# A two-layer fused kernel: which of two engines rounds to fp8 and splits the factors in its first phase

## The chip, the cores and the metric

The kernel runs on one core of a Trainium2 chip. The metric is the device time of one execution in microseconds; the median of three runs of the kernel before is 2216.24 us (2215.17 to 2216.98). The engines are named as in the profile: PE (TensorE, matrix products), DVE (VectorE), ACT (ScalarE), POOL (GpSimd) and SP (SyncE, which issues the DMAs here).

## The reference

x has 4 x 1024 rows of 1024 columns. Four sublayers follow one another, each with a residual: `x = x + tanh(g) * f(layernorm(x))`.

```python
# first: both operands are rounded to fp8, with a factor for each block
amax = max(|xb|) over 128 columns of a row          # 128x128 for ctx
q = (xb * (448 / safe)).astype(float8_e4m3fn)        # safe = max(amax, eps)
xq = q * (safe / 448)
out = einsum('emk,enk->emn', xq, wq)                 # wq: ctx, in the same way
# second: rms norm, 8-bit activations with one scale for all of x, ternary weights
# third: attention over 8 heads, with ctx as keys and values
# fourth: 8 experts of rank 128, the best two of each row are taken
```

## The kernel before

The work is cut into 32 tiles of 128 rows, 8 to a batch. A first phase does the first sublayer and prepares the weights; it has to be over before the second starts, since the second sublayer quantises with one maximum over all of x. The second phase does the other three sublayers. The edit touches only the first phase.

In the first phase one loop, `for j in range(FIRST, LAST + 1)` (from -12 to 33), is written out by hand for every engine: in turn j each engine does its steps for different tiles, in the order of its program, and semaphores join the engines. A tile n of x goes through these steps (`j + k` means that the step is done in turn j for tile j + k):

- SP loads it (j + 5). DVE takes mean and variance (`x_stats`, j + 4, L971 and L977), POOL makes the inverse deviation from these with two small operations (`x_rstd`, j + 4, L469 and L471), and ACT subtracts the mean (`centre`).
- DVE takes the maximum of each block of 128 columns and makes the factors from it (`x_max`, j + 3, L1007 to L1015). POOL makes the factors of the way back and splits them into a high and a low part (`x_factors`, j + 3, five operations on 8 columns, L476 to L484). ACT scales the eight blocks (`x_scale`).
- The rounding to fp8 is done in f32: a step is added and subtracted again. DVE (`x_round_start`, j + 2) masks the exponents (L982), makes the step of them (L985) and adds it (L987); POOL (`x_round`, j + 2, L490) subtracts it and writes f16. The step lies in one buffer, so the next tile's mask waits for POOL's subtraction.
- The rounded tile is multiplied by the high and the low part of its factors: ACT does the high half (`x_high`, j + 1), DVE the low one (`x_low`, j + 1, L1022). SP transposes both by DMA (`turn_x`, j + 1), PE multiplies (`product`), DVE adds the residual and takes the next statistics (`finish_x1`, j - 1, L1080). ACT and DVE take a maximum for the second sublayer (`x1_abs`, `x1_max`, L1087).

A tile of ctx goes the same way without statistics: `c_max` (j + 20, L1038), `c_scale` (ACT), `c_round_start` on DVE (j + 9, the same L982 to L987) and `c_round` on POOL (L496), `c_high` and `c_low` (both ACT, for the first batch `c_low` is DVE's, L1028). Three times, in turns -3, 5 and 13, DVE makes the factors of a batch of ctx (`c_factors`), for which it waits for PE. In turns 10 to 21 DVE reduces two tiles of weights (`weight_stat`, L1092), and from turn 24 on it rounds and splits the weights (`ternary_round`, `weight_low`). SP's order for a turn puts the loads of the weights ahead of `turn_x`, and these wait for `weight_stat` or `weight_low` of the same turn.

Of the kernel before, what the change touches and what calls it, by code (L numbers as in the profile page):

```python
# [9 lines left out]
KB = D // P  # L10
# [50 lines left out]
def flamingo_two_layers(nc, x, ctx_in, g_xattn, g_ffn, w0, gamma, router_w, wa, wb, out):  # L61
# [8 lines left out]
    with ExitStack() as stack:  # L70
# [69 lines left out]
        xd, xt1, xt2 = small(KB), small(KB), small(KB)  # L140
# [73 lines left out]
        x_d, x_hi, x_lo, x_turned = signal("x_d", 5), signal("x_hi"), signal("x_lo"), signals("x_turned", 2, 32)  # L214
# [239 lines left out]
        def _(pool):  # L454
# [18 lines left out]
            def x_factors(n):  # L473

                pool.wait_ge(x_am.sem, x_am.at(n, 2))
                pool.tensor_scalar(xd[:], xsafe[:, n % 2], -AMP / FP8_MAX, None, ALU.mult).then_inc(x_d.sem, 1)  # L476
                pool.wait_ge(x_d.sem, x_d.at(n, 1))
                pool.tensor_scalar(xt1[:], xd[:], SPLIT7, None, ALU.mult).then_inc(x_d.sem, 1)
                pool.wait_ge(x_d.sem, x_d.at(n, 2))
                pool.tensor_tensor(xt2[:], xt1[:], xd[:], ALU.subtract).then_inc(x_d.sem, 1)  # L480
                pool.wait_ge(x_d.sem, x_d.at(n, 3))
                pool.tensor_tensor(xdh[:, n % 4], xt1[:], xt2[:], ALU.subtract).then_inc(x_d.sem, 1)
                pool.wait_ge(x_d.sem, x_d.at(n, 4))
                pool.tensor_tensor(xdl[:, n % 4], xd[:], xdh[:, n % 4], ALU.subtract).then_inc(x_d.sem, 1)  # L484

            def x_round(n):
                pool.wait_ge(x_u.sem, x_u.at(n))
                after(pool, x_hi, n - 2)
                after(pool, x_lo, n - 2)
                pool.tensor_tensor(XQ[n % 2], XC[n % 3][:], XSTEP, ALU.subtract).then_inc(x_q.sem, 1)  # L490

            def c_round(m):
                pool.wait_ge(c_u.sem, c_u.at(m))
                after(pool, c_hi, m - 2)
                after(pool, c_lo, m - 2)
                pool.tensor_tensor(CQ[m % 2], C[m % 3], CSTEP, ALU.subtract).then_inc(c_q.sem, 1)  # L496
# [23 lines left out]
            for j in range(FIRST, LAST + 1):  # L520
                if is_x(j + 4):
                    x_rstd(j + 4)
                if is_x(j + 3):
                    x_factors(j + 3)
                if j in (-3, 5, 13):
                    c_tables((j + 11) // PER_BATCH)
                if j == PREP - 1:
                    weight_factors()
                if is_x(j + 2):
                    x_round(j + 2)  # L530
                if is_c(j + C_ROUND):
                    c_round(j + C_ROUND)
# [72 lines left out]
        def _(act):  # L605
# [23 lines left out]
            def x_high(n):  # L629
                act.wait_ge(x_q.sem, x_q.at(n))  # L630
                act.wait_ge(x_d.sem, x_d.at(n, 4))
                if n >= 2:
                    act.wait_ge(x_turned[n % 2].sem, x_turned[n % 2].at(n // 2 - 1))
                by_block(XHL[n % 2][0], XQ[n % 2], xdh[:, n % 4], x_hi)
# [334 lines left out]
        def _(dve):  # L969
# [9 lines left out]
            def round_start(v, s, v_sig, s_sig, u_sig, n):  # L979

                dve.wait_ge(v_sig.sem, v_sig.at(n))
                dve.tensor_scalar(s.bitcast(U16), v.bitcast(U16)[:, 1::2], EXP_MASK, None,  # L982
                                  ALU.bitwise_and).then_inc(s_sig.sem, 1)
                dve.wait_ge(s_sig.sem, s_sig.at(n, 1))
                dve.tensor_scalar(s, s, FP8_MIN_NORMAL, ROUND_FP8, ALU.max, ALU.mult).then_inc(s_sig.sem, 1)  # L985
                dve.wait_ge(s_sig.sem, s_sig.at(n))
                dve.tensor_tensor(v, v, s, ALU.add).then_inc(u_sig.sem, 1)  # L987

            def x_round_start(n):
                after(dve, x_q, n - 1)  # L990
                if n == 0:
                    dve.wait_ge(c_v.sem, c_v.at(PER_BATCH - 1))
                round_start(XC[n % 3][:], XSTEP, x_v, x_s, x_u, n)

            def c_round_start(m):
                after(dve, c_q, m - 1)
                round_start(C[m % 3], CSTEP, c_v, c_s, c_u, m)
# [19 lines left out]
            def x_low(n):  # L1017
                dve.wait_ge(x_q.sem, x_q.at(n))
                dve.wait_ge(x_d.sem, x_d.at(n))
                if n >= 2:  # L1020
                    dve.wait_ge(x_turned[n % 2].sem, x_turned[n % 2].at(n // 2 - 1))
                dve.tensor_tensor(blocks(XHL[n % 2][1]), blocks(XQ[n % 2]), spread(xdl[:, n % 4]), ALU.mult)\  # L1022
                   .then_inc(x_lo.sem, 1)
# [121 lines left out]
            for j in range(FIRST, LAST + 1):  # L1145
# [3 lines left out]
                if is_x(j + 1):  # L1149
                    x_low(j + 1)  # L1150
                if is_x(j + 3):
                    x_max(j + 3)
                if is_x(j + 4):
# [5 lines left out]
                if is_x(j + 2):  # L1159
                    x_round_start(j + 2)  # L1160
                if j in (-3, 5, 13):
                    c_factors((j + 11) // PER_BATCH)
                if is_c(j + C_ROUND):
                    c_round_start(j + C_ROUND)
# [222 lines left out]
```

## Time and profile before

| what | value |
|---|---|
| median of three runs | 2216.24 us |
| the profiled execution | 2218.67 us |
| its span | 2216.9 us |
| busy in the span: PE | 1866.9 us (84%) |
| DVE | 1668.4 us (75%) |
| ACT | 1360.1 us (61%) |
| POOL | 858.3 us (39%) |
| end of the first phase | about 607 us |

Busy time is the time in which an instruction is under way on an engine, its waiting for a memory port included; waiting for a semaphore counts as idle time. The times of a timeline start at the span's start.

### The profile page before, as it was taken

To read this page: it belongs to the slowest core of one execution; us is meant where nothing else is said; L and a number is where in the kernel's file an instruction comes from. 1 tells how busy PE (TensorE), PEld (TensorE's weight loads), DVE (VectorE), ACT (ScalarE), POOL (GpSimd) and SP (SyncE) were. 2 spreads that over 40 slices of the span, in tenths; PEclk is the share of its full clock that TensorE was granted. 3 is DMA by queue.
4 is the path that set the end of the run, shared out by engine and by line. 5 is a ranking of instruction groups with operands and counts; after the bars stand their busy time and mean duration, and the time that the engine had idled before them with its cause. 6 is when DMAs were issued, how large, how long until landed. Compare 5 with 4: busy or idle time off the path is not lost.

```text
span 2216.9 us, 26479 instructions
## 1 busy us (share of the span) xinstructions
PE 1866.9 (84%) x8716; PEld 826.1 (37%) x8716; DVE 1668.4 (75%) x2348; ACT 1360.1 (61%) x2587; POOL 858.3 (39%) x1256
## 2 busy tenths in 40 slices
PE   0186667777746999999999999999999999999997
PEld 0032223332312444444444444444444444444443
DVE  8999989999546777777767777777777767777661
ACT  5798969977225565565565565565565565565650
POOL 2666646654023333333333433333333333433320
PEclk9998887898967999999999999999999999999998
DMA  7778769978637778878888878788778878778781
GB/s 217 193 208 198 199 176 233 250 182 213 183 92 140 150 154 170 159 156 168 158 156 165 161 162 163 158 162 161 161 155 168 158 156 163 164 163 163 133 150 41
DMA packets 963529, 369.33 MB, mean 167 GB/s; under 512 B 915136, under 2 KB 931520, under 8 KB 963392
## 3 DMA queue, kind: packets, MB, share of 16 engines
q1 hardware_dynamic: 963392, 367.64, 76.7%
q8 instruction: 69, 1.13, 0.2%
q14 instruction: 68, 0.56, 0.1%
HBM read 105.42 MB, written 33.55 MB: 63 GB/s over the span
## 4 chain that ended last, share of the span: by engine, by line
DVE 38%; issue 17%; ACT 16%; PE 13%; POOL 9%; DMA 6%; SPq 1%; POOLq 0%; ACTq 0%; DVEq 0%
ACT slot L716 7%; DVE tiny L971 7%; DVE tiny L1240 7%; POOL tiny L572 4%; ACT arena L708 4%; DMA slot<-slot 3%; POOL tiny L570 3%; DVE slot L1244 3%; ACT tiny L702 2%; PE accs L848 2%; PE sc L865 2%; PE accs L850 2%; PE accs L849 2%; DMA probs<-slot 2%; DVE slot L1022 2%
## 5 line engine op out<-in xcount | busy, mean ns | idle before, releaser
L1244 DVE SCALAR_TENSOR_TENSOR slot<-arena,tiny,slot 128x1024 f16<-128x1024 f32 x256 | 328.2, 1282 | 283.2 <-ACT slot L716 283.1
L865 PE MATMUL sc<-arena,slot 128*128 128x512 f16 x1536 | 381.3, 385 | 31.0 <-ACT arena L708 21.3
L716 ACT ACTIVATE slot<-arena,tiny 128x1024 f16<-128x1024 f32 x256 | 293.7, 1147 | 182.0 <-POOL tiny L572 166.6
L570 POOL TENSOR_SCALAR tiny<-tiny 128x1 f32<-128x1 f32 x256 | 99.3, 388 | 704.5 <-ACT arena L708 704.5
L1240 DVE TENSOR_REDUCE tiny<-sc 128x1 f32<-128x1024 f32 x256 | 308.5, 1206 | 57.8 <-PE sc L865 57.8
L708 ACT ACTIVATE arena<-sc,tiny,head_tab 128x1024 f32<-128x1024 f32 x256 | 308.4, 1205 | 8.6
L702 ACT ACTIVATE tiny<-tiny,head_tab 128x1 f32<-128x1 f32 x256 | 74.1, 289 | 359.4 <-DVE tiny L1240 358.4
L810 PE MATMUL sc<-probs,slot 128*128 128x512 f16 x768 | 190.0, 412 | 89.1 <-DMA slot<-slot 78.9
L865 PEld LDWEIGHTS sc<-arena,slot 128*128 128x128 f16 x1536 | 151.2, 99 | 219.7 <-ACT arena L708 25.9
L810 PE MATMUL sc<-wa_hi,slot 128*128 128x512 f16 x512 | 145.8, 406 | 78.1 <-DMA wa_lo<-wb_lo 46.8
L848 PE MATMUL accs<-wb_hi,slot 128*128 128x512 f16 x512 | 195.1, 381 | 7.5 <-DMA slot<-slot 7.5
L848 PE MATMUL accs<-wa_hi,slot 128*128 128x512 f16 x512 | 199.7, 390 | 0.0
L850 PE MATMUL accs<-wa_hi,slot 128*128 128x512 f16 x512 | 199.4, 389 | 0.0
L849 PE MATMUL accs<-wa_lo,slot 128*128 128x512 f16 x512 | 199.0, 389 | 0.0
L881 PE MATMUL accs<-probs,arena 128*128 128x512 f16 x512 | 195.0, 381 | 4.1 <-issue 3.9
L849 PE MATMUL accs<-wb_lo,slot 128*128 128x512 f16 x512 | 195.0, 381 | 0.0
L850 PE MATMUL accs<-wb_hi,slot 128*128 128x512 f16 x512 | 194.8, 380 | 0.0
L883 PE MATMUL accs<-probs,arena 128*128 128x512 f16 x512 | 194.8, 380 | 0.0
L882 PE MATMUL accs<-probs,arena 128*128 128x512 f16 x512 | 194.6, 380 | 0.0
L572 POOL TENSOR_TENSOR tiny<-tiny,neg_one 128x1 f32<-128x1 f32 x256 | 161.3, 630 | 21.3
L810 PEld LDWEIGHTS sc<-probs,slot 128*128 128x128 f16 x768 | 79.0, 105 | 199.4 <-DMA slot<-slot 85.3
L612 ACT ACTIVATE wb_lo<-wb_lo,slot 128x128 f16<-128x128 f16 x448 | 136.2, 386 | 14.7 <-POOL wb_lo L496 12.9
(178 smaller groups left out, 3181.0 us busy)
## 6 DMA issues: line engine op xcount, KB each, us to landing
wb_hi<-in_ctx SPq DMA_DIRECT2D x36, 512.0 KB, 4.7
arena<-in_x SPq DMA_DIRECT2D x32, 512.0 KB, 3.6
x_scratch<-arena SPq DMA_DIRECT2D x32, 512.0 KB, 3.1
slot<-x_scratch SPq DMA_DIRECT2D x32, 512.0 KB, 3.8
slot<-in_ctx SPq DMA_DIRECT2D x32, 512.0 KB, 4.1
out<-arena SPq DMA_DIRECT2D x32, 512.0 KB, 3.4
slot<-in_L_ffn_weight SPq DMA_DIRECT2D x16, 512.0 KB, 3.4
slot<-in_L_ffn_Wa SPq DMA_DIRECT2D x16, 512.0 KB, 4.8
```

What stands on the lines that cost most here:

```text
L572: pool.tensor_tensor(rinv[c % 2][:], rsum[c % 2][:], neg_one[:], ALU.pow).then_inc(s_ri.sem, 1)
L708: act.activation(PF[c % 2], sc[:, c % 2, :], ACT.Exp, bias=nbias[c % 2][:], scale=head_tab[:, n, 1:2], accum_out=rsum[c % 2][:]).then_inc( ...
L716: act.activation(PH[c % 2], PF[c % 2], ACT.Identity, scale=rinv[c % 2][:]).then_inc(s_ph.sem, 1)
L810: mm = pe.matmul(sc[:, j % 2, h * HALF:(h + 1) * HALF], lhs[:, cols], rhs[:, k, h * HALF:(h + 1) * HALF], start=start, stop=stop)
L848: pe.matmul(accs[:, a, :], lhs_hi, r_hi[:, k, cols], start=k == 0, stop=False)
L849: pe.matmul(accs[:, a, :], lhs_hi, r_lo[:, k, cols], start=False, stop=False)
L850: mm = pe.matmul(accs[:, a, :], lhs_lo, r_hi[:, k, cols], start=False, stop=k == KB - 1)
L865: mm = pe.matmul(sc[:, c % 2, h * HALF:(h + 1) * HALF], q[i][:, c * P:(c + 1) * P], k[j][:, h * HALF:(h + 1) * HALF], start=start, stop=stop)
L881: pe.matmul(accs[:, ACC_V, :], v[0][:, cols], PT[:, h, j, :], start=j == 0, stop=False)
L883: mm = pe.matmul(accs[:, ACC_V, :], v[1][:, cols], PT[:, h, j, :], start=False, stop=j == KB - 1)
L1240: dve.tensor_reduce(nmx[c % 2][:], sc[:, c % 2, :], AX.X, ALU.max, negate=True).then_inc(s_mx.sem, 1)
L1244: dve.scalar_tensor_tensor(out=PL[c % 2], in0=PF[c % 2], scalar=rinv[c % 2][:], in1=PH[c % 2], op0=ALU.mult, op1=ALU.subtract).then_inc(s_ ...
```

## The change

- Both passes of each rounding are POOL's: the addition of the step goes from DVE (L987) to POOL, ahead of the subtraction, for x and for ctx. DVE keeps the mask and the step.
- The low half of x (`x_low`) goes from DVE to POOL.
- The factors of x (`x_factors`) go from POOL to DVE, behind `x_max`. There are four instructions instead of five, since two of them do two steps each.
- The order within a turn is changed on both engines. On DVE: the steps of x and ctx first (with `c_factors` between them), then `x_max` and `x_factors`, `x_stats`, `x1_max`, the rest as before. On POOL: `x_low`, `x_round`, `x_rstd`, the tables of ctx, `c_round`.

```diff
 (POOL)
+            def x_low(n):
+                pool.wait_ge(x_q.sem, x_q.at(n))
+                pool.wait_ge(x_d.sem, x_d.at(n))
+                if n >= 2:
+                    pool.wait_ge(x_turned[n % 2].sem, x_turned[n % 2].at(n // 2 - 1))
+                pool.tensor_tensor(blocks(XHL[n % 2][1]), blocks(XQ[n % 2]), spread(xdl[:, n % 4]), ALU.mult)\
+                    .then_inc(x_lo.sem, 1)
             def x_round(n):
+                pool.wait_ge(x_s.sem, x_s.at(n))
+                pool.tensor_tensor(XC[n % 3][:], XC[n % 3][:], XSTEP, ALU.add).then_inc(x_u.sem, 1)
                 pool.wait_ge(x_u.sem, x_u.at(n))
...
             def c_round(m):
+                pool.wait_ge(c_s.sem, c_s.at(m))
+                pool.tensor_tensor(C[m % 3], C[m % 3], CSTEP, ALU.add).then_inc(c_u.sem, 1)
                 pool.wait_ge(c_u.sem, c_u.at(m))
...
             for j in range(FIRST, LAST + 1):
+                if is_x(j + 1):
+                    x_low(j + 1)
+                if is_x(j + 2):
+                    x_round(j + 2)
                 if is_x(j + 4):
                     x_rstd(j + 4)
-                if is_x(j + 3):
-                    x_factors(j + 3)
                 if j in (-3, 5, 13):
                     c_tables((j + 11) // PER_BATCH)
                 if j == PREP - 1:
                     weight_factors()
-                if is_x(j + 2):
-                    x_round(j + 2)
                 if is_c(j + C_ROUND):
                     c_round(j + C_ROUND)
 (DVE)
-            def round_start(v, s, v_sig, s_sig, u_sig, n):
+            def rounding_step(v, s, v_sig, s_sig, n):
...
-                dve.wait_ge(s_sig.sem, s_sig.at(n))
-                dve.tensor_tensor(v, v, s, ALU.add).then_inc(u_sig.sem, 1)
...
+            def x_factors(n):
+                dh, dl = xdh[:, n % 4], xdl[:, n % 4]
+                dve.tensor_scalar(xd[:], xsafe[:, n % 2], -AMP / FP8_MAX, None, ALU.mult).then_inc(x_d.sem, 1)
+                dve.wait_ge(x_d.sem, x_d.at(n, 1))
+                dve.scalar_tensor_tensor(out=xt2[:], in0=xd[:], scalar=SPLIT7, in1=xd[:], op0=ALU.mult,
+                                         op1=ALU.subtract).then_inc(x_d.sem, 1)
+                dve.wait_ge(x_d.sem, x_d.at(n, 2))
+                dve.scalar_tensor_tensor(out=dh, in0=xd[:], scalar=SPLIT7, in1=xt2[:], op0=ALU.mult,
+                                         op1=ALU.subtract).then_inc(x_d.sem, 1)
+                dve.wait_ge(x_d.sem, x_d.at(n, 3))
+                dve.tensor_tensor(dl, xd[:], dh, ALU.subtract).then_inc(x_d.sem, 1)
...
-                if is_x(j + 1):
-                    x_low(j + 1)
+                if is_x(j + 2):
+                    x_step(j + 2)
+                if j in (-3, 5, 13):
+                    c_factors((j + 11) // PER_BATCH)
+                if is_c(j + C_ROUND):
+                    c_step(j + C_ROUND)
                 if is_x(j + 3):
                     x_max(j + 3)
+                    x_factors(j + 3)
                 if is_x(j + 4):
                     x_stats(j + 4)
                 if is_x(j - 2):
                     x1_max(j - 2)
                 if j == PREP - 1:
                     weight_factors()
-                if is_x(j + 2):
-                    x_round_start(j + 2)
-                if j in (-3, 5, 13):
-                    c_factors((j + 11) // PER_BATCH)
-                if is_c(j + C_ROUND):
-                    c_round_start(j + C_ROUND)
                 if is_x(j - 1):
                     finish_x1(j - 1)
```

## Rows read from the trace of the kernel before

**Rows 1.** Busy us by stretch: PE, weight load, DVE, ACT, POOL, then clock, DMA.
```profile
200.00:250.00 50.00, 36.98 (x158) 15.58 (x157) 48.82 (x71) 46.59 (x141) 34.71 (x33) 0.92 0.89 222
607.00:2216.90 1609.90, 1489.32 (x7170) 667.23 (x7170) 1117.74 (x1548) 905.46 (x1281) 547.95 (x930) 0.97 0.77 152
```

**Rows 2.** Timeline of one pass, DVE and one POOL row: start us, us, engine, operation.
```profile
201.16 1.22 DVE L987 TENSOR_TENSOR wb_hi<-wb_hi,slot 128x1024 f32<-128x1024 f32 x1
202.31 1.28 DVE L1080 SCALAR_TENSOR_TENSOR arena<-sc,tiny,arena 128x1024 f32<-128x1024 f32 x1
...
205.07 2.12 POOL L496 TENSOR_TENSOR wb_lo<-wb_hi,slot 128x1024 f16<-128x1024 f32 x1
206.15 2.13 DVE L1022 TENSOR_TENSOR slot<-slot 128x1024 f16<-128x1024 f16 x1
208.20 1.21 DVE L1007 TENSOR_REDUCE tiny<-slot 128x8 f32<-128x1024 f32 x1
...
210.08 1.28 DVE L971 BATCH_NORM_STATS2 tiny<-arena 128x6 f32<-128x512 f32 x2
...
211.52 1.17 DVE L1087 CUSTOM_DVE_ANT_0 slot<-slot 128x1024 f32<-128x1024 f32 x1
...
216.15 1.22 DVE L987 TENSOR_TENSOR wb_hi<-wb_hi,slot 128x1024 f32<-128x1024 f32 x1
```

**Rows 3.** Timeline of the same pass on ACT.
```profile
205.18 1.15 ACT L663 ACTIVATE slot<-arena,row_tab 128x1024 f32<-128x1024 f32 x1 [0.20 <-DVE row_tab L977]
206.24 2.43 ACT L612 ACTIVATE slot<-slot 128x128 f16<-128x128 f16 x8
208.57 2.43 ACT L612 ACTIVATE wb_lo<-wb_lo,slot 128x128 f16<-128x128 f16 x8
```

**Rows 4.** Groups of instructions by line, 100 to 550 us: busy us, mean ns.
```profile
L490 POOL TENSOR_TENSOR slot<-slot,arena 128x1024 f16<-128x1024 f32 x29 | 61.8, 2130 | 0.3 <-issue 0.2
...
L982 DVE TENSOR_SCALAR arena<-slot 128x1024 uint16<-128x1024 uint16 x29 | 20.3, 701 | 0.0
...
L985 DVE TENSOR_SCALAR arena<-arena 128x1024 bf16<-128x1024 bf16 x29 | 12.4, 427 | 1.0
...
L1066 DVE SCALAR_TENSOR_TENSOR slot<-slot 128x64 f32<-128x64 f32 x2 | 0.5, 226 | 0.1
```

**Rows 5.** Timeline of DVE and POOL at three places.
```profile
96.06 2.74 DVE L1028 TENSOR_TENSOR wb_lo<-wb_lo,slot 128x1024 f16<-128x1024 f16 x1
97.68 3.10 POOL L496 TENSOR_TENSOR wb_lo<-wb_hi,slot 128x1024 f16<-128x1024 f32 x1
98.73 3.14 DVE L1022 TENSOR_TENSOR slot<-slot 128x1024 f16<-128x1024 f16 x1
...
184.66 2.12 POOL L490 TENSOR_TENSOR slot<-slot,arena 128x1024 f16<-128x1024 f32 x1
184.68 2.38 DVE L985 TENSOR_SCALAR slot<-slot 128x1024 bf16<-128x1024 bf16 x1
...
464.88 1.75 DVE L1109 TENSOR_SCALAR slot<-slot,tiny 4x128 f32<-4x128 f32 x1
```

**Rows 6.** Groups of instructions by line on POOL, whole span.
```profile
L551 POOL TENSOR_TENSOR slot<-slot 128x1024 f16<-128x1024 f32 x32 | 73.2, 2289 | 70.4 <-ACT slot L726 70.4
```

**Rows 7.** Timeline of DVE: `finish_x1` of tiles 0, 21 and 27, and `c_factors` in pass 13.
```profile
123.54 1.28 DVE L1080 SCALAR_TENSOR_TENSOR arena<-sc,tiny,arena 128x1024 f32<-128x1024 f32 x1
...
317.43 0.23 DVE L1053 TENSOR_SCALAR slot<-accs 128x64 f32<-128x64 f32 x1 [7.42 <-PE accs L800]
...
461.65 1.28 DVE L1080 SCALAR_TENSOR_TENSOR arena<-sc,tiny,arena 128x1024 f32<-128x1024 f32 x1
...
547.26 1.28 DVE L1080 SCALAR_TENSOR_TENSOR arena<-sc,tiny,arena 128x1024 f32<-128x1024 f32 x1 [0.80 <-PE sc L810]
```

**Rows 8.** Timeline of DVE: sums of two ctx tiles ahead of x.
```profile
36.09 1.23 DVE L987 TENSOR_TENSOR wb_hi<-wb_hi,slot 128x1024 f32<-128x1024 f32 x1
...
41.70 1.22 DVE L987 TENSOR_TENSOR wb_hi<-wb_hi,slot 128x1024 f32<-128x1024 f32 x1
```

More of the change, by code:

```diff
@@ L139, in flamingo_two_layers @@
         xam, xsafe, xrec, xk = small(KB), sb("xsafe", [P, 2, KB]), small(KB), sb("xk", [P, 2, KB])
-        xd, xt1, xt2 = small(KB), small(KB), small(KB)
+        xd, xt2 = small(KB), small(KB)
         xdh, xdl = (slot[13][:, 192 + i * 32:224 + i * 32].rearrange("p (a k) -> p a k", a=4) for i in range(2))
@@ L213, in flamingo_two_layers @@
                                          signal("x_q"))
-        x_d, x_hi, x_lo, x_turned = signal("x_d", 5), signal("x_hi"), signal("x_lo"), signals("x_turned", 2, 32)
+        x_d, x_hi, x_lo, x_turned = signal("x_d", 4), signal("x_hi"), signal("x_lo"), signals("x_turned", 2, 32)
         mm1, e_x1, x1_out, e_st, e_abs, e_max = (signal("mm1"), signal("e_x1"), signal("x1_out", 16), signal("e_st", 3),
@@ L471, in x_rstd @@
                 pool.tensor_tensor(xrstd[:, i:i + 1], xa_[:], neg_half[:, 0:1], ALU.pow).then_inc(x_rs.sem, 1)
[L473 to L484, printed above, removed]
+            def x_low(n):
[5 more added lines that the diff above has]
+                    .then_inc(x_lo.sem, 1)
             def x_round(n):
+                pool.wait_ge(x_s.sem, x_s.at(n))
+                pool.tensor_tensor(XC[n % 3][:], XC[n % 3][:], XSTEP, ALU.add).then_inc(x_u.sem, 1)
                 pool.wait_ge(x_u.sem, x_u.at(n))
@@ L630, in x_high @@
                 act.wait_ge(x_q.sem, x_q.at(n))
-                act.wait_ge(x_d.sem, x_d.at(n, 4))
+                act.wait_ge(x_d.sem, x_d.at(n, 3))
                 if n >= 2:
@@ L985, in round_start, with x_step @@
                 dve.tensor_scalar(s, s, FP8_MIN_NORMAL, ROUND_FP8, ALU.max, ALU.mult).then_inc(s_sig.sem, 1)
-                dve.wait_ge(s_sig.sem, s_sig.at(n))
-                dve.tensor_tensor(v, v, s, ALU.add).then_inc(u_sig.sem, 1)
-            def x_round_start(n):
+            def x_step(n):
                 after(dve, x_q, n - 1)
@@ L992, in x_round_start, with c_step @@
                     dve.wait_ge(c_v.sem, c_v.at(PER_BATCH - 1))
-                round_start(XC[n % 3][:], XSTEP, x_v, x_s, x_u, n)
-            def c_round_start(m):
+                rounding_step(XC[n % 3][:], XSTEP, x_v, x_s, n)
+            def c_step(m):
                 after(dve, c_q, m - 1)
-                round_start(C[m % 3], CSTEP, c_v, c_s, c_u, m)
+                rounding_step(C[m % 3], CSTEP, c_v, c_s, m)
             def x_stats(n):
@@ L1015, in x_max @@
                 dve.tensor_scalar(xk[:, i], xrec[:], xrstd[:, i:i + 1], FP8_MAX, ALU.mult, ALU.mult).then_inc(x_k.sem, 1)
[L1017 to L1023, printed above, removed]
+            def x_factors(n):
[9 more added lines that the diff above has]
+                dve.tensor_tensor(dl, xd[:], dh, ALU.subtract).then_inc(x_d.sem, 1)
             def c_low(m):
```

## The prediction

> **What bounds the kernel now.** I read the busy time by stretch first. The edit touches only the first phase, the first 607 us of the span. In 200 to 250 us DVE is busy 48.8 of 50 us, ACT 46.6, POOL 34.7 and PE 37.0 [rows 1]: DVE sets the pace and ACT is close behind. In the second phase, which the edit leaves as it is, DVE is busy 1117.7 of 1609.9 us [rows 1]; a gain or a loss of the first phase therefore moves the end one for one.
>
> Then the timeline of one pass. By pass j I mean one turn of the loop over j. From sum to sum of a ctx tile (L987 at 201.16 and at 216.15) a pass takes 14.99 us, and DVE's pieces fill it [rows 2]: ctx sum 1.15, `finish_x1` and `c_max` together 3.84 (202.31 to 206.15), `x_low` 2.05, `x_max` 1.88, `x_stats` 1.44, `x1_max` 1.10, and the rounding of x and ctx up to 216.15. ACT's pass has five groups of eight block scalings, 2.33 us apart, and two operations of some 1.06 us [rows 3]: 5 x 2.33 + 2.1 = 13.8 us. That is the floor to which a faster DVE could bring the pass, 1.2 us below today.
>
> Last, and decisive here, how DVE and POOL stand in each other's way. At 184.64 DVE had just written the step of a ctx tile. Between its two step instructions there is a gap of some 0.03 us. POOL started its difference in it (184.66, 2.12 us), and DVE's next instruction, which takes 0.43 us alone [rows 4], took 2.38, ending 0.28 after POOL [rows 5]. In the group from 96 us the two take turns: DVE's L1028 ends at 98.80, POOL's L496, begun at 97.68, takes 3.10 instead of some 2.13, and DVE's L1022, begun at 98.73, takes 3.14 and ends 1.09 after it [rows 5]. Even 128 elements on four partitions wait: L1109 took 1.75 us beside POOL's L496 [rows 5]. Instructions of another kind don't wait: POOL's L496 at 205.07 lies beside `c_max`, and DVE gets to its next instruction, L1022, at 206.15 as ever; that one then stands for POOL and ends 1.09 after it [rows 2]. So the wait is not a slowing of both; one stands until the other's instruction is through.
>
> The Trainium skill ("SBUF — State Buffer", Who interferes with whom) says the same of two kinds of DVE instruction, those in a two-port mode and those with two SBUF inputs: each and a GpSimd operation exclude one another for a whole instruction. By that rule a `tensor_scalar` of 8 elements waits too, which no row here shows; by it my sum stands, without it a pass would be some 0.9 us shorter (below).
>
> **What the change moves, per pass.** From DVE go two sums (1.15 each) and `x_low` (2.05, of which some 0.9 is waiting for POOL); to it come four instructions on 8 columns, some 0.25 us apart as those on 64 columns (0.23 each) [rows 2, 4]. DVE's own work: 14.99 - 2.3 - 2.05 + 1.0 = 11.7 us, rounded up for the last spacing. From POOL go five small operations; to it come three large ones. No row shows POOL doing these three; its large two-tensor operations take 2.13 us (L490) and 2.29 (L551, with waiting) [rows 4, 6], so I take 2.1 from start to start. The f16 input and the spread factor of `x_low` may make it dearer; 2.29 each is my upper end, 2.1 the lower one. POOL's pass: 5 x 2.13 + the pair of `x_rstd`, about 0.9 = 11.6 us. Each engine alone would be faster than ACT's 13.8. What decides is the order in which they exclude one another.
>
> **A pass of the changed kernel, walked.** Clock 0 is the end of `x_stats`, for which POOL's `x_rstd` waits, and behind it in POOL's order everything else.
> - 0 to 1.1: DVE's `x1_max`. POOL's `x_rstd` pair stands behind it and ends at 1.8. DVE goes on with `finish_x1` and `c_max` to 4.95 (from pass 10 with two weight statistics to 7.2), which POOL doesn't disturb. POOL: ctx sum 1.9 to 4.0, ctx difference 4.1 to 6.2.
> - DVE's first mask (x) waits for it: 6.2 to 6.85. In the gap behind it POOL's `x_low` enters: 6.9 to 8.95. DVE scales the step 9.0 to 9.4 and runs straight into the ctx mask, to 10.05. Here POOL's x sum enters, 10.05 to 12.2. DVE's ctx scale: to 12.6.
> - DVE's block maximum runs beside POOL's x difference (12.6 to 14.7), but `xsafe` waits for its end. Then seven small instructions, 14.7 to 16.4, and `x_stats` to 17.8.
>
> So 17.8 us a pass: DVE's 11.7 and 6 us of standing for POOL (1.2 + 2.1 + 2.1 + 1.0, less rounding). ACT has 4 us to spare in it, PE more. The weight statistics of passes 10 to 21 are hidden: they fall where DVE would wait anyway.
>
> **The sum.** `finish_x1` of tile 0 is at 123.54, of tile 21 at 461.65, of tile 27 at 547.26 [rows 7].
> - 21 passes between the first two, 338.1 us now. Nineteen become 17.8. In pass 5 `c_factors` adds some 2.7 of its own: 20.5. In pass 13 DVE waits for PE at `c_factors` until 317.43 (7.42 of it idle) [rows 7], some 15.3 behind the end of pass 12, as the transposes are issued only behind the weight statistics of that pass. `c_factors` now stands ahead of `x_max`, so more is left behind it: 15.3 + 2.7 + 11.5 = 29.5, against 27.4 now and against 17.8: 30.6 with the shift of phase. Together 19 x 17.8 + 20.5 + 30.6 = 389.3: +51.
> - Six passes to tile 27, 85.6 us now. No ctx tile is rounded any more. The first takes 16.2, the second 12.2; the four with weights: 13.2 of DVE's work, and 3.0 waiting for POOL's x sum and difference at `x_max` = 16.2. Together 93.2: +7.6.
> - Before tile 0: ctx alone takes 5.61 a pass (36.09 to 41.70) [rows 8]. Now: step 1.15, sum 2.1, difference 2.2, and `c_low` 1.1 between these two = 6.5; five passes, +4.5. Passes -2 to 0, 43.4 us together in the timeline now, become by the same walk 17.6, 17.6 (with `c_low` on DVE) and 16.5: +8.3. Passes -4 and -3, where the ctx step and `c_factors` now stand ahead of x's statistics, so that these come later and `x_rstd` with all behind it on POOL waits: +5, an estimate from the same walk. Together +18.
> - The last four tiles wait for transposes and PE, whose place behind `weight_low` in SP's order doesn't change: 0, give or take 3.
>
> Sum +76.5 us. Before's profiled execution took 2218.67 us with a span of 2216.9 and some 1.8 around it, 2.4 above the median of 2216.24; I put the change on the median: 2292.7, rounded 2292.
>
> **Bounds.** If the three new operations of POOL cost 2.29 instead of 2.1, a pass gains 0.2 for each: 28 passes x 0.6 = +16. If small instructions of 8 columns with one input don't wait, -0.9 x 27 = -24. If each of the 28 passes has one handover less than I walked (2.1 us), -59: 2233. If it has half of one more, +29: 2321.
>
> **The rivals.**
> - **The pair is packed well** (0.13). The order falls so that DVE's own long work (6.4 us of statistics and maxima) covers POOL. Then only the sum of what excludes one another counts: 5 x 2.13, 0.5 of `x_rstd`, four step instructions 2.3, `x1_max` 1.1, the small ones 1.1 = 15.6 a pass, against 15.2 on average: 27 x 0.4 = +11: 2227. Against it: `x_rstd` stands ahead of the ctx rounding in POOL's order, so POOL idles 3 us in each pass, and DVE's step instructions stand in a row.
> - **The other side: the relief counts** (0.08). DVE gets its turn without waiting for more than 2 us a pass, 11.7 + 2.1 = 13.8, ACT's floor. 20 passes x 1.2 less, the rest unchanged: 2192. It decides from the point where DVE's waits stay under 3.3 us a pass. For it: DVE's busy time today. Against it: rows 5, in which a single gap cost 1.95 us.
> - **The three operations are dearer than any of POOL's today** (0.12), for instance by 0.5 each, 28 passes x 1.5 = +42 more: 2334.
> - **It changes nothing that can be told** (0.02): waits and relief cancel, 2216.
> - My forecast: 0.65.
>
> Measured medians of this kernel lie within 0.1%; 0.2% is what can be told from no change. Slower by more: 0.65 + 0.12 + 0.13 less 0.01 = 0.89; same 0.03; faster 0.08. The range, 2232 to 2326, leaves out the gain and the dearest case.
>
> **What would show it.** In the timeline of the changed kernel: passes of 17 to 18 us in mid phase; the bfloat16 scalings of the step (0.43 alone) at some 2 us on average; POOL's five large operations some 2.1 each, with POOL idle ahead of `x_rstd`; `xsafe` behind the end of POOL's x difference; DVE's busy share still high, as its waits are booked as busy; the second phase as long as before. I'm wrong if the scalings keep 0.43 us, or if a pass takes less than 15 us.

## The result and the profile after

The changed kernel took 2255.11 us (median of four runs, 2244.87 to 2257.19), the kernel before 2216.61 on the same chip (2215.17 to 2218.73): 1.0171 times as long, with a 95% interval of 1.0149 to 1.0192. It is slower, as forecast; the loss of 38.5 us is half of the 76 forecast. The profiled execution took 2254.88 us, its span is 2253.1, 36.2 longer than before's 2216.9.

Busy time by stretch, as in [rows 1]: the same 50 us, and the second phase.

```profile
200.00:250.00 50.00, 28.99 (x111) 11.69 (x110) 48.82 (x69) 41.60 (x126) 37.96 (x25) 0.80 0.70 172
645.50:2253.10 1607.60, 1484.66 (x7171) 666.16 (x7170) 1120.23 (x1552) 904.37 (x1281) 543.80 (x930) 0.97 0.77 152
```

DVE is still booked as busy for 48.82 of 50 us, though three of its large instructions a pass are gone. ACT fell from 46.59 to 41.60 and PE from 36.98 to 28.99: less work goes through in the same time. So what counts as DVE's busy time is to a good part standing. One pass on DVE shows where; it answers to [rows 2], from the end of one `x_stats` over the LayerNorm statistics behind `finish_x1` (256.70) to the next `x_stats` (L981 is the mask, L984 the scaling of a step, L1004 to L1025 the block maximum and the factors).

```profile
254.17 0.21 DVE L976 BATCH_NORM_AGGREGATE xmv<-tiny 128x2 f32<-128x12 f32 x1
...
256.70 1.29 DVE L970 BATCH_NORM_STATS2 tiny<-arena 128x6 f32<-128x512 f32 x2
...
258.15 1.17 DVE L1040 TENSOR_REDUCE slot<-wb_hi 128x8 f32<-128x1024 f32 x1
259.23 1.83 DVE L981 TENSOR_SCALAR arena<-slot 128x1024 uint16<-128x1024 uint16 x1
261.10 2.00 DVE L984 TENSOR_SCALAR arena<-arena 128x1024 bf16<-128x1024 bf16 x1
263.02 0.68 DVE L981 TENSOR_SCALAR slot<-wb_hi 128x1024 uint16<-128x1024 uint16 x1
263.73 2.23 DVE L984 TENSOR_SCALAR slot<-slot 128x1024 bf16<-128x1024 bf16 x1
265.89 1.20 DVE L1004 TENSOR_REDUCE tiny<-slot 128x8 f32<-128x1024 f32 x1
267.13 0.86 DVE L1008 TENSOR_SCALAR xsafe<-tiny 128x8 f32<-128x8 f32 x1
...
268.26 0.23 DVE L1012 TENSOR_SCALAR xk<-tiny 128x8 f32<-128x8 f32 x1
268.40 0.16 DVE L1017 TENSOR_SCALAR tiny<-xsafe 128x8 f32<-128x8 f32 x1
268.60 0.17 DVE L1019 SCALAR_TENSOR_TENSOR tiny<-tiny 128x8 f32<-128x8 f32 x1
...
269.08 1.28 DVE L970 BATCH_NORM_STATS2 tiny<-arena 128x6 f32<-128x512 f32 x2
270.40 0.21 DVE L976 BATCH_NORM_AGGREGATE xmv<-tiny 128x2 f32<-128x12 f32 x1
```

And the same pass on POOL: `x_rstd` (L469, L471), ctx sum and difference (L491, L495), `x_low` (L478), x sum and difference (L483, L487).

```profile
254.46 1.08 POOL L469 TENSOR_SCALAR tiny<-xmv 128x1 f32<-128x1 f32 x1 [2.74 <-DVE xmv L976]
...
256.16 2.14 POOL L491 TENSOR_TENSOR wb_hi<-wb_hi,slot 128x1024 f32<-128x1024 f32 x1
258.37 2.14 POOL L495 TENSOR_TENSOR wb_lo<-wb_hi,slot 128x1024 f16<-128x1024 f32 x1
260.46 2.35 POOL L478 TENSOR_TENSOR slot<-slot 128x1024 f16<-128x1024 f16 x1
263.17 2.51 POOL L483 TENSOR_TENSOR slot<-slot,arena 128x1024 f32<-128x1024 f32 x1 [0.36 <-DVE arena L984]
265.76 2.20 POOL L487 TENSOR_TENSOR slot<-slot,arena 128x1024 f16<-128x1024 f32 x1
```

Read them side by side. POOL's L495 ends at 260.51, and the mask, begun at 259.23, ends only at 261.06: 1.83 us instead of 0.68. Behind it POOL's `x_low` is through first, and the scaling of x's step takes 2.00 instead of 0.43. The second mask slips in at its own 0.68; then POOL's x sum gets its turn, and the scaling of the ctx step takes 2.23. The block maximum is undisturbed (1.20), and `xsafe`, on 8 columns, stands for POOL's L487 until 267.96. These four stand for 1.15 + 1.57 + 1.80 + 0.63 = 5.15 us in a pass of 16.23, from one end of `x_stats` (254.38) to the next (270.61). Before, one instruction a pass stood, `x_low`, for 0.92 (2.13 in [rows 2] where it takes 1.21 undisturbed), and from pass 10 on, where the weight statistics lie ahead of `x_low`, none. This is no single pass: the groups, 100 to 550 us, answer to [rows 4].

```profile
L984 DVE TENSOR_SCALAR slot<-slot 128x1024 bf16<-128x1024 bf16 x24 | 49.9, 2080 | 0.8
L984 DVE TENSOR_SCALAR arena<-arena 128x1024 bf16<-128x1024 bf16 x26 | 41.5, 1596 | 0.9
L981 DVE TENSOR_SCALAR arena<-slot 128x1024 uint16<-128x1024 uint16 x26 | 34.9, 1342 | 0.0
L1008 DVE TENSOR_SCALAR xsafe<-tiny 128x8 f32<-128x8 f32 x27 | 22.3, 827 | 1.0
```

Last, `finish_x1` of tiles 0, 21 and 27, and `c_factors` of pass 13, beside [rows 7].

```profile
136.85 1.25 DVE L1082 SCALAR_TENSOR_TENSOR arena<-sc,tiny,arena 128x1024 f32<-128x1024 f32 x1
...
343.18 0.22 DVE L1055 TENSOR_SCALAR slot<-accs 128x64 f32<-128x64 f32 x1 [13.92 <-PE accs L799]
...
499.44 1.28 DVE L1082 SCALAR_TENSOR_TENSOR arena<-sc,tiny,arena 128x1024 f32<-128x1024 f32 x1
...
588.03 1.28 DVE L1082 SCALAR_TENSOR_TENSOR arena<-sc,tiny,arena 128x1024 f32<-128x1024 f32 x1
```

| stretch | before, us | after, us | difference | forecast |
|---|---|---|---|---|
| start of the span to tile 0 | 123.5 | 136.9 | +13.3 | +18 |
| tile 0 to 21 | 338.1 | 362.6 | +24.5 | +51 |
| tile 21 to 27 | 85.6 | 88.6 | +3.0 | +7.6 |
| tile 27 to 31 | 56.8 | 57.5 | +0.8 | 0 |
| tile 31 to the end | 1612.9 | 1607.5 | -5.4 | 0 |

The last line is not the edit's. In the ten further kernels below, whose second phase is the same code, it took 1603.9 to 1611.1 us in one execution each. Before's 1612.9 is the longest of all.

### The profile page after: what moved, and what is told of

Read it like the earlier page. It is cut to its first block, busy times and chain, and to the rows that moved or that the text cites. A ratio compares the mean times of both kernels' runs of the same rounds, so it can differ in the third digit from the quotient of the medians.

```text
span 2253.1 us, 26447 instructions
## 1 busy us (share of the span) xinstructions
PE 1866.8 (83%) x8716; PEld 825.8 (37%) x8716; DVE 1689.4 (75%) x2380; ACT 1357.6 (60%) x2587; POOL 956.1 (42%) x1192
## 4 chain that ended last, share of the span: by engine, by line
DVE 37%; issue 19%; ACT 16%; PE 12%; POOL 9%; DMA 6%; SPq 1%; POOLq 0%; ACTq 0%; DVEq 0%
ACT slot L715 7%; DVE tiny L1241 7%; DVE tiny L970 7%; POOL tiny L571 4%; ACT arena L707 4%; DMA slot<-slot 3%; POOL tiny L569 3%; DVE slot L1245 2%; ACT tiny L701 2%; DMA probs<-slot 2%; PE sc L864 2%; DVE arena L1253 2%; DVE slot L1228 2%; PE sc L809 2%; PE accs L847 2%
## 5 line engine op out<-in xcount | busy, mean ns | idle before, releaser
L611 ACT ACTIVATE slot<-slot,xk 128x128 f32<-128x128 f32 x256 | 78.2, 388 | 119.0 <-DVE xk L1012 119.0
```

## The experiments

Theory A is the prediction's: DVE and POOL exclude one another for a whole instruction, and what a pass loses is set by which of POOL's operations is ready in the gaps between DVE's short ones. Theory B: POOL's added work by itself makes the loss, wherever it stands. Theory C: neither; the new order with its chain of handed-over results costs what it costs through waits for data. D and E came up on the way and are told where they are tested. The table is the ledger of all of them, from one steady pass each, `finish_x1` to `finish_x1` around 200 to 265 us: "standing" is the sum of what DVE's instructions took above their undisturbed duration in the same kernel, "own" is the rest of the pass, without idle time. The last column compares with runs of the kernel before on the same chip.

| kernel | pass | own | standing, and on what | median, us | ratio to before, 95% |
|---|---|---|---|---|---|
| before | 14.98 | 14.06 | 0.92: `x_low` | | |
| after | 16.23 | 11.08 | 5.15: mask, both scalings, `xsafe` | 2255.11 | 1.0171 [1.0149, 1.0192] |
| a1, sums back on DVE | 16.17 | 13.61 | 2.56: mask, ctx scaling | 2252.21 | 1.0166 [1.0135, 1.0196] |
| a2, `x_low` back on DVE | 15.76 | 12.22 | 3.54: `x_low`, ctx scaling, `xsafe` | 2246.23 | 1.0136 [1.0117, 1.0156] |
| a3, masks first | 15.99 | 10.83 | 5.16: both masks, `xsafe`, `xk` | 2253.40 | 1.0174 [1.0136, 1.0213] |
| a4, one block of eight on POOL | 13.76 | 11.18 | 0; 2.58 idle for ACT | 2170.91 | 0.9799 [0.9775, 0.9823] |
| a5, order of before | 15.32 | 11.10 | 4.22: ctx scaling, `xsafe`, `xk` | 2221.73 | 1.0041 [1.0028, 1.0054] |
| b1, before in the new order | 15.86 | 14.05 | 1.81: ctx scaling | 2247.32 | 1.0141 [1.0118, 1.0164] |
| b2, before with `x_low` later | 14.09 | 14.09 | 0 | 2202.40 | 0.9952 [0.9935, 0.9969] |
| b3, b2 with the x sum on POOL | 14.61 | 12.82 | 1.79: `xsafe` | 2203.32 | 0.9956 [0.9942, 0.9970] |
| w1, b3's division, grouped | 14.24 | 12.90 | 0; 1.34 idle for ACT | 2236.69 | 1.0111 [1.0078, 1.0144] |
| w2, after's division, grouped | 16.97 | 11.19 | 3.17: `xk`, one factor; 2.61 idle for ACT | 2272.82 | 1.0271 [1.0236, 1.0305] |

In passes 14 to 21, with two weight statistics in each, the same count gives 15.2 and nothing standing for before, 12.2 and 4.0 for the changed kernel, 15.2 and 1.8 for b1, 12.2 and 3.1 for a5, 15.2 and nothing for b2.

### Is it POOL's length, or the order alone? (a4, b1)

The first takes nearly all the length out of POOL's five large operations and leaves order and semaphores of the changed kernel. Seven blocks of eight of each result are left out; the time alone is of use.

```diff
-pool.tensor_tensor(XC[n % 3][:], XC[n % 3][:], XSTEP, ALU.add)
+pool.tensor_tensor(XC[n % 3][:, 0:P], XC[n % 3][:, 0:P], XSTEP[:, 0:P], ALU.add)
 ...
```

> The changed kernel with all five large POOL operations of a turn (both sums, both differences, x_low) cut to one block of 128 columns of 1024; order, semaphores and DVE's work stay. Left out: seven blocks of eight of each of these results (they are zero or unrounded). Theory A and B: passes fall to ACT's floor of 13.8 us, 2171 us (2160 to 2185). Theory C (the new order or its semaphores cost the time, whatever POOL's operations last): a pass stays at 15 us or more, above 2205 us.

2170.91 us, as expected. The busy times of 200 to 250 us:

```profile
200.00:250.00 50.00, 37.62 (x156) 15.76 (x154) 43.16 (x85) 50.00 (x154) 14.19 (x26) 0.86 0.91 239
```

ACT is busy all the time and sets the pass, 13.8 us, the floor that [rows 3] gave. Theory C is out: the same order with the same semaphores, but short operations on POOL, doesn't hold a pass above ACT's floor. A and B had the same number here.

The second leaves POOL and DVE what they have in the kernel before and gives both the changed kernel's order.

```diff
 for j ...:      # DVE's loop; on POOL x_round and x_factors go ahead of x_rstd
+    if is_x(j + 2): x_round_start(j + 2)
+    if j in (-3, 5, 13): c_factors((j + 11) // PER_BATCH)
+    if is_c(j + C_ROUND): c_round_start(j + C_ROUND)
     if is_x(j + 3): x_max(j + 3)
 ...
-    if is_x(j + 2): x_round_start(j + 2)
-    if j in (-3, 5, 13): c_factors((j + 11) // PER_BATCH)
-    if is_c(j + C_ROUND): c_round_start(j + C_ROUND)
```

> The kernel before with its own division of the work (DVE adds the steps and does x_low, POOL the factors), but with the order of the changed kernel on DVE and POOL: steps first, then the maxima and statistics; x_round ahead of x_rstd. Theory A: POOL's x difference is now ready while DVE is between ctx mask and ctx scale, about 1.9 us of waiting, against the 0.9 us that x_low waited: passes of 15.6 us (from pass 12 on 16.8) against 15.0 and 15.2: 2246 us (2235 to 2255). Theory B (POOL's load, DVE's relief): no operation has changed sides, so 2216 us, within 5.

2247.32 us: A's number, and most of the changed kernel's loss, without one operation more on POOL than before. B is refuted as the main cause. The place, DVE and POOL (L490 is POOL's x difference, L982 and L985 mask and scaling of the ctx step):

```profile
250.41 0.69 DVE L982 TENSOR_SCALAR slot<-wb_hi 128x1024 uint16<-128x1024 uint16 x1
250.57 2.51 POOL L490 TENSOR_TENSOR slot<-slot,arena 128x1024 f16<-128x1024 f32 x1 [4.56 <-DVE slot L987]
251.13 2.23 DVE L985 TENSOR_SCALAR slot<-slot 128x1024 bf16<-128x1024 bf16 x1
...
262.81 1.22 DVE L1022 TENSOR_TENSOR slot<-slot 128x1024 f16<-128x1024 f16 x1
```

The difference, asked for at 250.57 during the mask, gets in between mask and scaling, and the scaling takes 2.23 instead of 0.43. `x_low` has lost its wait in exchange (262.81, 1.22). One handover of 0.92 was traded for one of 1.81; in the passes with weight statistics, 15.2 us before, it is the whole 1.8: 17.0.

### Undoing one part at a time (a1, a2)

```diff
 def rounding_step(v, s, v_sig, s_sig, u_sig, n):    # a1, on DVE
 ...
+    dve.wait_ge(s_sig.sem, s_sig.at(n))
+    dve.tensor_tensor(v, v, s, ALU.add).then_inc(u_sig.sem, 1)
 # and both sums deleted on POOL
```

> The changed kernel, but DVE adds the step again (both sums back on DVE), so that DVE's own work per pass is 13.9 us and POOL's falls by 4.2. Theory A (DVE and POOL exclude one another; what counts is which POOL operation is ready at the gaps between DVE's short locked instructions): the x difference now enters the gap between ctx mask and ctx scale (about 1.9 us of waiting) and x_low stands before the x mask (about 0.9), so a pass is 16.2 to 16.5 us, as long as with the sums on POOL: 2253 us (2245 to 2262). Theory B (POOL's load is the cause): most of the loss goes with the two sums, 2215 to 2225.

2252.21 us; the interval includes the changed kernel's ratio. POOL is relieved of 4.3 us a pass and DVE burdened with 2.3, and the pass moves by 0.06: own work +2.5, standing -2.6. Once more B's number (2215 to 2225) is far off.

```diff
-if is_x(j + 1): x_low(j + 1)     # head of POOL's loop
+if is_x(j + 1): x_low(j + 1)     # head of DVE's loop (a2)
```

> The changed kernel, but x_low is DVE's again, at the head of its turn. Theory A: DVE does 1.1 us more, one handover of about 2 us at the x step is gone; walked by the same rules a pass is 15.7 us against 16.2: 2244 us (2238 to 2250). Theory B (load): POOL loses one of five large operations, a third of the loss: 2242 us. Not meant to tell these two apart, but to size one handover.

2246.23 us, 2.2 over the expected. Own work +1.14, standing -1.61: the pass is 0.5 shorter, 15.76 where 15.7 was expected. Neither part of the division alone is the culprit. B had 2242 here, so this run doesn't tell the two apart; it sizes one handover.

### Can the gaps be avoided? (a3)

Theory D: the loss sits in the gap between mask and scaling; with both masks ahead of both scalings, it shrinks.

```diff
     x_mask(j + 2)
     c_mask(j + C_ROUND)
+    x_scale_step(j + 2)
+    c_scale_step(j + C_ROUND)
```

> The changed kernel with DVE's four step instructions in the order mask x, mask ctx, scale x, scale ctx, so that no instruction waits for the one just ahead of it and the four run without a gap (2.1 us in one piece). Theory A (POOL's operations only change place: x_low, x sum and x difference still have to run between the step and the statistics, now in the gaps between the small instructions on 8 columns): a pass is 16.5 us against 16.2, 2261 us (2250 to 2268). Theory D (the gaps between the step instructions are the fault): without them about 4 us a pass go, down to ACT's floor, below 2205 us.

2253.40 us: not told apart from the changed kernel, and D's number (under 2205) missed by some 50. The scalings run at 0.41 to 0.42, but the ctx mask (L981) takes 2.38 and `xk` (L1014), on 8 columns, 1.93:

```profile
259.15 1.82 DVE L981 TENSOR_SCALAR arena<-slot 128x1024 uint16<-128x1024 uint16 x1
260.38 2.35 POOL L478 TENSOR_TENSOR slot<-slot 128x1024 f16<-128x1024 f16 x1
260.90 2.38 DVE L981 TENSOR_SCALAR slot<-wb_hi 128x1024 uint16<-128x1024 uint16 x1
...
266.01 2.12 POOL L487 TENSOR_TENSOR slot<-slot,arena 128x1024 f16<-128x1024 f32 x1
266.24 1.93 DVE L1014 TENSOR_SCALAR xk<-tiny 128x8 f32<-128x8 f32 x1
```

The standing is 5.16 against 5.15: it has only moved. A had 2261 and passes of 16.5; the time lies in its range, the pass took 15.99. And the gap isn't needed. The ctx mask began at 260.90, before the x mask was through (260.97), and still stood for `x_low`, which had been standing since 260.38. Here an operation of POOL that stood already got in behind the DVE instruction it stood for, without a gap.

### The order of before with the new division (a5)

Theory E: the order alone makes the loss; then this one, with the new division in the old order, is as fast as the kernel before.

```diff
 # POOL's and DVE's loops as in the kernel before, operations as in the changed one
-    x_round(j + 2)                                       # POOL, ahead of x_rstd(j + 4)
+    x_round(j + 2)                                       # POOL, behind weight_factors
-    x_step(j + 2); c_factors(...); c_step(j + C_ROUND)   # DVE, ahead of x_max(j + 3)
+    x_step(j + 2); c_factors(...); c_step(j + C_ROUND)   # DVE, behind weight_factors
```

> The division of the changed kernel (sums and x_low on POOL, factors on DVE) in the order of the kernel before, on both engines. It completes a square of two divisions and two orders. Theory A, walked: the step instructions are through before POOL's x sum, but POOL's five large operations then run in a row to 14.0 us after x_stats, and DVE's small instructions wait for two of them: 16.0 us a pass; with the slower ctx passes at the start (6.5 against 5.6) 2244 us (2236 to 2255). Theory E (the loss of the changed kernel is that of its order alone, as b1 lost 31 us by the order alone): 2216 us, within 6.

2221.73 us, seven runs. With b1 this closes a square:

| | order of before | order of the change |
|---|---|---|
| division of before | 1 | 1.0141 |
| division of the change | 1.0041 | 1.0171 |

The order costs 1.3 to 1.4 per cent in either row; the division 0.4 in the old order. In the new one 0.3, which the intervals of b1 and of the changed kernel don't tell apart. The traces say the same: `finish_x1` of tile 31 is at 604.0 us before, 636.0 in b1, 614.2 in a5 and 645.6 in the changed kernel, so that the order costs 32.0 and 31.3 us and the division 10.2 and 9.6, in one execution each. So three quarters to four fifths of the loss come from the order, 29 to 32 us. "Order" is both engines' at once; the share of each wasn't tried. In a5 `x_low` and the factors stay where the changed kernel has them, since before has no place for them on these engines. E's number (2216, within 6) is just met, though this kernel is told apart from before. My own by A, 2244, was wrong by 22. I had walked 16.0 us; a pass takes 15.32, and 15.3 to 15.8 with weight statistics. DVE and POOL (L983 to L491 as in the changed kernel):

```profile
250.32 2.51 POOL L483 TENSOR_TENSOR slot<-slot,arena 128x1024 f32<-128x1024 f32 x1
250.88 2.23 DVE L984 TENSOR_SCALAR slot<-slot 128x1024 bf16<-128x1024 bf16 x1
...
258.11 1.30 DVE L1008 TENSOR_SCALAR xsafe<-tiny 128x8 f32<-128x8 f32 x1
259.34 1.90 POOL L478 TENSOR_TENSOR slot<-slot 128x1024 f16<-128x1024 f16 x1
259.69 1.58 DVE L1012 TENSOR_SCALAR xk<-tiny 128x8 f32<-128x8 f32 x1
```

Here `x_low` begins at 259.34, in the gap behind `xsafe`, and `xk` on 8 columns stands for it. Own work is the changed kernel's 11.1. Against before, in the same order, the new division takes 3.0 us of own work off DVE and puts 3.3 of standing on it. Against the changed kernel, what differs is that POOL's x difference, its ctx sum and the first part of its ctx difference (252.91 to 259.39, one behind the other) lie beside `finish_x1`, its statistics, `c_max` and the block maximum (253.03 to 258.08), and one standing less is left.

### Moving one step of the kernel before (b2, b3)

If the place decides, before's own 0.92 can be had without any new division: `x_low` goes behind `x_stats`, where POOL has nothing large left.

```diff
 ...                                     # POOL's x_factors also waits for its own last one
-                if is_x(j + 1):
-                    x_low(j + 1)
                 if is_x(j + 3):
                     x_max(j + 3)
                 if is_x(j + 4):
                     x_stats(j + 4)
+                if is_x(j + 1):
+                    x_low(j + 1)
```

> The kernel before with one step moved: DVE does x_low behind x_stats instead of at the head of its turn. No operation changes its engine or its length alone. Theory A: x_low no longer meets POOL's ctx difference, which now lies beside the block maxima; passes up to 9 fall from 15.0 to 14.1 us, those with weight statistics (where x_low didn't wait) stay at 15.2: 2204 us (2198 to 2211). Theory B (load): nothing, 2216 us.

2202.40 us over ten runs, against 2204 expected: faster than both kernels, and with b3 below, which can't be told from it, the fastest that computes the whole. Busy times and the pass (L491, L497 POOL's differences; L1008 block maximum; L1023 `x_low`):

```profile
200.00:250.00 50.00, 38.28 (x162) 16.44 (x163) 48.76 (x76) 49.12 (x150) 37.50 (x31) 0.90 0.90 231
```

```profile
213.19 2.13 POOL L491 TENSOR_TENSOR slot<-slot,arena 128x1024 f16<-128x1024 f32 x1
214.12 1.29 DVE L972 BATCH_NORM_STATS2 tiny<-arena 128x6 f32<-128x512 f32 x2
215.27 2.13 POOL L497 TENSOR_TENSOR wb_lo<-wb_hi,slot 128x1024 f16<-128x1024 f32 x1
215.56 1.17 DVE L1039 TENSOR_REDUCE slot<-wb_lo 128x8 f32<-128x1024 f32 x1
216.65 1.21 DVE L1008 TENSOR_REDUCE tiny<-slot 128x8 f32<-128x1024 f32 x1
...
219.97 1.21 DVE L1023 TENSOR_TENSOR slot<-slot 128x1024 f16<-128x1024 f16 x1
```

Both of POOL's large operations lie whole beside statistics and maxima, which take their usual time; `x_low` takes 1.21. Nothing of DVE's stands. In passes 14 to 21 a pass takes the 15.2 it took before, where nothing stood. With ACT at 49.12 of 50 us the next bound is reached too.

b3 gives POOL the x sum on top of that, to use DVE's undisturbed time further.

```diff
 # on top of b2; the x sum is deleted on DVE
+                pool.wait_ge(x_s.sem, x_s.at(n))                      # x_round(n) on POOL
+                pool.tensor_tensor(XC[n % 3][:], XC[n % 3][:], XSTEP, ALU.add)
 ...
-                if is_x(j + 2): x_round(j + 2)     # POOL's loop, ahead of c_round
+                if is_x(j + 2): x_round(j + 2)     # behind it
```

> b2 (the kernel before with x_low behind x_stats), and x's sum moved to POOL, where x_round now comes behind c_round, so that nothing of POOL's large work is ready before DVE's step instructions are through. Theory A: in passes with weight statistics DVE's 15.3 us fall by the sum's 1.15 and POOL's three operations (6.4 us) fit beside DVE's statistics and maxima: 14.3 us against 15.2; passes up to 9 stay at 14.1 to 14.3 (ACT's floor, and 1.4 us of waiting at xsafe): 2192 us (2185 to 2200). Theory B (each large operation moved to POOL costs): above 2202 us, the time of b2.

2203.32 us, no gain over b2, where 2192 was expected; B's number, above 2202, is met. The trace shows three things against it. In passes up to 9, `xsafe` waits for POOL's x difference (1.79), which the sum ahead of it has made later: own work -1.27, standing +1.79. In the passes with weight statistics ACT waits for that difference:

```profile
379.27 2.14 POOL L493 TENSOR_TENSOR slot<-slot,arena 128x1024 f16<-128x1024 f32 x1
380.93 0.50 DVE L1015 TENSOR_SCALAR xsafe<-tiny 128x8 f32<-128x8 f32 x1
381.44 2.44 ACT L615 ACTIVATE slot<-slot 128x128 f16<-128x128 f16 x8 [0.77 <-POOL slot L493]
```

Three large operations, 6.4 us, no longer fit beside the 5.05 us from the start of `finish_x1` to the end of the block maximum (b2: 212.81 to 217.86). Even so b3 gains 5.6 us on b2 from tile 0 to 21 (327.7 against 333.3). It loses 6.3 from tile 21 to 27 (89.2 against 82.8), where DVE waits twice for PE at the summary of the weights, 1.85 and 2.13 us; the rest of that stretch is not explained.

### Gathering all of DVE's undisturbed work (w1, w2)

In both kernels I put statistics and maxima in one run behind `finish_x1`, with POOL's large operations in one run beside them, and moved ACT's scalings to match. w1 has before's division with x's sum on POOL, as b3, and w2 the changed one.

```diff
 # DVE, tail of the loop; ahead of finish_x1 come c_factors, the ctx step and the x step
+    x_stats(j + 4); x_max(j + 3); x_low(j + 1); x1_max(j - 2)     # w1
+    x_stats(j + 4); x_max(j + 3); x_factors(j + 3); x1_max(j - 2) # w2
 # ACT: x_scale(j + 3) and centre(j + 4) moved behind the work on ctx
```

> The division of before, save that x's sum is POOL's, in an order made from theory A: DVE does ctx step and sum, x step, then all that doesn't exclude POOL in one stretch (finish_x1, ctx maximum or weight statistics, x_stats, block maximum), then the small ones, x_low and x1_max; POOL does x sum, x difference, ctx difference inside that stretch, then x_rstd and the factors; on ACT x_scale and centre go to the end of the turn. Theory A: DVE's work is 12.6 to 13.9 us a pass with little waiting, so ACT's floor of 13.8 to 14 decides: 2184 us (2176 to 2195). Theory B (every further large operation on POOL costs): above 2216 us.

> The division of the changed kernel (both sums and x_low on POOL, factors on DVE) in the same kind of order as w1. POOL's five large operations take 10.4 us in a row and meet DVE's small instructions at the end of its stretch. Theory A: 15.0 us a pass, with ctx alone 6.5 against 5.6 as in the changed kernel: 2216 us (2205 to 2228), 39 us less than the changed kernel by order alone, but no gain on before. Theory B: still near 2255 us.

Both missed, by 53 and 57 us: 2236.69 and 2272.82. In w1 nothing stands for POOL, and its steady pass is the expected 14.2. But the mask waits for ACT in each pass, and `c_factors` for PE's transposes (before: 7.4 us in all, in pass 13 [rows 7]):

```profile
200.39 0.69 DVE L986 TENSOR_SCALAR arena<-slot 128x1024 uint16<-128x1024 uint16 x1 [1.34 <-ACT slot L616]
```

```profile
L1058 DVE TENSOR_SCALAR slot<-accs 128x64 f32<-128x64 f32 x2 | 0.5, 225 | 23.3 <-PE accs L804 23.3
```

Its passes 5 and 13 take 29.9 and 32.4 us, where before has 19.8 and 29.5. In w2 the same wait for ACT is 2.6 us a pass, and two small instructions stand besides, for 3.2 us:

```profile
246.31 0.69 DVE L982 TENSOR_SCALAR arena<-slot 128x1024 uint16<-128x1024 uint16 x1 [2.61 <-ACT slot L612]
...
254.37 1.83 DVE L1013 TENSOR_SCALAR xk<-tiny 128x8 f32<-128x8 f32 x1
256.31 1.74 DVE L1020 SCALAR_TENSOR_TENSOR tiny<-tiny 128x8 f32<-128x8 f32 x1
```

But most of w1's loss lies later. It reaches tile 21 only 1.3 us behind before (462.9 against 461.7) and takes 166.9 from there to tile 31, against 142.4: `finish_x1` waits for PE, 40.4 us in all against 18.2 before, 34.9 of it from 480 us on. In w2 the same stretch takes 162.4, against 146.1 in the changed kernel. Which part of the order makes PE late wasn't tried. An order that is right for the pair DVE and POOL can be wrong for ACT and PE. B's number for w1, above 2216, is met as well, yet nothing of DVE's stands for POOL in its steady pass; w2's fits neither. So these two decide nothing between A and B, and give no gain.

## Why the prediction was right, and by what its size was off

**The bound.** Right. The loss of the first phase, 41.6 us up to `finish_x1` of tile 31, reached the end but for 5.4, which is within what the second phase varies by between executions of the same code (1603.9 to 1612.9).

**What the change moves.** DVE's own work was put at 11.7 us a pass and is 11.08. About half of that is the spacing of the small instructions: on 8 columns they start 0.20 apart (268.40, 268.60) and take 0.17, not the 0.25 taken from those on 64 columns, and the four add 0.68 and not 1.0. Most of the rest is that each sum took the gap ahead of it along: from the start of a scaling to the next mask it was 1.60 before (213.36 to 214.96) and is 0.35 without the standing, 1.25 less where 1.15 had been taken off.

**Whether small instructions wait.** No row of before showed it, and the forecast had it by the nearest, the 128 elements of [rows 5]. The trace now shows it for 8 columns: `xsafe` 0.86, in a5 `xk` 1.58, in a3 1.93, against 0.23 alone.

**The walk.** All handovers are where it put them: the mask behind POOL's ctx difference, `x_low` between mask and scaling, x sum behind the ctx mask, x difference beside the block maximum and `xsafe` behind it. Even POOL's idle time ahead of `x_rstd` is there, 2.74 against some 3. With clock 0 at the end of `x_stats` (254.38):

| end of | walk | trace |
|---|---|---|
| `x_rstd` | 1.8 | 1.81 |
| ctx difference | 6.2 | 6.13 |
| `x_low` | 8.95 | 8.43 |
| x sum | 12.2 | 11.30 |
| x difference | 14.7 | 13.58 |
| last small instruction (start of `x_stats`) | 16.4 | 14.70 |
| `x_stats` | 17.8 | 16.23 |

So the step that was off is the price of a handover, in "a pass of the changed kernel, walked". The walk let DVE stand for 1.2, 2.1, 2.1 and 1.0 us (6.4, where the sum has 6); the mask, the two scalings and `xsafe` stood for 1.15, 1.57, 1.80 and 0.63. I had let each instruction start anew, 2.1 us for POOL's operation and 0.4 for DVE's scaling behind it. But one that stood needs less than its whole time from the other's end: `x_low` ends 1.75 us after DVE's mask, where alone it takes 1.90 (a5, 259.34), x sum and difference 1.98 and 2.00 after DVE's end where 2.12 was their time in [rows 5]; the scaling of the ctx step ends 0.28 after POOL's. [Rows 5] had that last number, for L985, and I quoted it and walked with 0.4 all the same. With the rest of the walk this splits the 1.57 us between 17.8 and 16.23 so: 17.8 was 11.7 of own work and 6.1 of standing, 16.23 is 11.08 and 5.15. Standing makes 0.95 of it (0.2 of which is that `x_low` takes 1.90 even undisturbed, not 2.1), own work 0.6. The passes of 17 to 18 us that were to be seen in mid phase were therefore not seen.

**The sum.** The two passes with `c_factors` and the two behind them took 86.0 us together, forecast 86.7. The other 17 between tiles 0 and 21 took 276.6, where 17.8 each makes 302.6: the 26 us too much of this term. The wait for PE in pass 13 grew from 7.42 to 13.92, as the argument on `c_factors` had it. Ahead of tile 0 the ctx passes were right (6.45 us from mask to mask, 6.5 forecast); the 4.7 too much lie, by subtraction, in the passes with x, which have the same handovers; I did not go through them one by one. From tile 21 to 27, four passes with weights took 60.3 where I had 64.8. In the first of them (527.75 to 543.38) DVE stood for 2.5 us, not 3.0; but the last took 13.75 where I had 16.2, and that one I did not go through.

**The bounds.** The large operations were not dearer (2.12 undisturbed, `x_low` 1.90), and "one handover less", 2233, did not come about; the truth was the same number of handovers, each cheaper, which was none of my cases. That the range held 2255 is partly luck: its lower end was made for a case that did not occur.

**The rivals.** "The pair is packed well" was refuted for this order (15.6 a pass) and is what a5 shows, at 15.32. "The relief counts" fell: DVE's waits were to stay under 3.3 us and are 5.15. What I hadn't seen is that the order, and not the division, carries most of the loss; the prediction argued from both at once, and didn't walk them apart.

## What to carry to other kernels

Where two engines exclude one another for whole instructions, keep a ledger of one pass: own work, standing, idle time, and for each standing the other engine's operation behind it. Then place the other engine's long operations beside work that doesn't exclude them, before moving any work across: moving one step gave 0.5%, while moving three large operations (with a new order) lost 1.7%. Busy time hides all this, as a standing instruction is booked as busy; compare each instruction's duration with its shortest one. And a new order has to be walked for every engine that hands over to it, not for the two in question alone.

## What the runs showed of the hardware that was not expected

- An instruction that stood ends sooner behind the other's end than its whole time. DVE's 0.43-us scaling ends 0.28 us after POOL's operation; POOL's 1.90-us `x_low` ends 1.75 after DVE's.
- Which side gets in is a matter of hundredths of a microsecond. In the changed kernel `x_low`, standing since 260.46, got in behind the mask that ended at 261.06, and in a3 it did so although DVE's next mask had begun (260.90) before the end of the one ahead (260.97). The ctx mask at 263.02 ran at its 0.68 all the same: it began before the end of the scaling ahead of it (263.10), and POOL's x sum needs that scaling's result, so that it came at 263.17 and took 2.51 instead of 2.12.
- The size of the standing instruction is no protection: 8 columns took 1.93 instead of 0.23. The Trainium skill ("SBUF — State Buffer", Who interferes with whom) says "Issue order, not op shape, decides who blocks"; these rows agree.
- POOL's two-tensor operation on 128x1024 takes 2.12 us, DVE's 1.23. The Trainium skill ("GPSIMD Engine Reference", 3.1 Elementwise — side-by-side cycle accounting) gives a ratio of 1.96 at 2048 float32 elements; here, at 1024 and with a bfloat16 step as second input, it is 1.7.

What stays open: why the second phase of one execution differs by up to 9 us between kernels with the same code there, and whether a third arrangement would bring ACT's floor of 13.8 us with the new division. That wasn't tried.
